# Two layers of attention and experts: blended rows, a third group of expert tiles, respaced preparation, router earlier

## The reference, cut to what matters

```python
# layer 0: causal linear attention (16 heads of 8) and a mixture of 8 experts, 2 of them per token
xn = layernorm(x)
q, k, v = xn @ Wq.T, xn @ Wk.T, xn @ Wv.T           # rope, then elu + 1 on q and k
y_t = (q_t @ sum_{i<=t} k_i v_i^T) / max(q_t . sum_{i<=t} k_i, eps)
p = softmax(xn @ router_w.T); top two, weights normalised
x = x + y @ Wo.T + sum_e w_e * square(relu(xn @ fc_e.T)) @ proj_e.T + shared expert
# layer 1: softmax attention in chunks of 64 with a gate, and a token-shift feed-forward
xn = layernorm(x)
probs = softmax(q k^T / sqrt(8)), reweighed by a gate that is worked out from their sum
x_prev = xn shifted by one token, the first row zero
xr = mu_r * xn + (1 - mu_r) * x_prev
xk = mu_k * xn + (1 - mu_k) * x_prev
out = sigmoid(xr @ W_r.T) * (square(relu(xk @ W_k.T)) @ W_v.T)
x = x + attention + out
```

## Time and profile before

| | |
|---|---|
| median of the three runs | 1634.32 us (1632.23 to 1635.02) |
| the profiled execution's own time | 1633.0 us |
| its span, first to last instruction | 1631.0 us |
| mean granted TensorE clock | 0.972 of full speed |
| busy, share of the span | PE 89%, DVE 73%, ACT 49%, POOL 34% |
| first layer | 0 to about 542 us |
| expert tiles | about 542 to 850 us |
| second layer | about 850 to 1631 us |

### The profile page before, as it was taken

The page is one execution under the profiler, slowest core; times in us unless marked ns, Lnnn a source line. Parts: engine busy times, 40 slices in busy tenths (PEclk is TensorE's granted clock), DMA queues, the critical chain, the costliest instruction groups (busy, mean ns, idle before and its releaser), DMA issues.

```text
span 1631.0 us, 35341 instructions
## 1 busy us (share of the span) xinstructions
PE 1453.1 (89%) x13152; PEld 942.7 (58%) x13152; DVE 1193.0 (73%) x2666; ACT 800.3 (49%) x1505; POOL 548.2 (34%) x967
## 2 busy tenths in 40 slices
PE   3898998998997799997987899999999999999993
PEld 2666766766665699996973444444444444444441
DVE  4788788788787474464665688888888888888741
ACT  2344444444442333343324566666666666666672
POOL 2432332332322011351116043444444534452123
PEclk9999999999998999999997999999999999999996
DMA  4111111111111576776861444343444443432400
GB/s 113 41 41 47 48 41 47 47 41 47 41 34 43 160 218 213 234 227 181 243 155 54 86 97 86 87 89 85 83 105 105 99 96 80 90 83 54 85 8 13
DMA packets 117035, 152.86 MB, mean 94 GB/s; under 512 B 28788, under 2 KB 81652, under 8 KB 112244
## 3 DMA queue, kind: packets, MB, share of 16 engines
q1 hardware_dynamic: 103944, 120.25, 30.0%
q0 software_dynamic: 12928, 30.43, 6.1%
HBM read 109.01 MB, written 41.09 MB: 92 GB/s over the span
## 4 chain that ended last, share of the span: by engine, by line
PE 48%; DVE 26%; DMA 8%; POOL 6%; issue 5%; ACT 4%; SPq 3%; POOLq 0%; DVEq 0%; ACTq 0%
PE bank L1853 8%; PE bank L1844 8%; DVE P L1139 7%; DMA QT<-shift 6%; DVE nmax L1424 6%; PE bank L1721 5%; PE bank L1892 4%; PE bank L1917 4%; PE bank L1678 2%; PE bank L1755 2%; PE bank L1663 2%; PE bank L1966 2%; PE bank L1862 2%; PE bank L1769 2%; ACT QT L777 1%
## 5 line engine op out<-in xcount | busy, mean ns | idle before, releaser
L1424 DVE TENSOR_REDUCE nmax<-bank 128x1 f32<-128x512 f32 (+3 forms) x704 | 429.5, 632 | 116.7 <-PE bank L1892 110.6
L891 ACT ACTIVATE P<-bank 128x512 f32<-128x512 f32 x640 | 368.8, 597 | 284.6 <-PE bank L1917 282.2
L1892 PE MATMUL bank<-KT,QT 76*128 76x512 bf16 (+3 forms) x1024 | 255.6, 306 | 44.8 <-DVE nmax L1424 40.3
L1917 PE MATMUL bank<-QT,KT 78*128 78x512 bf16 (+3 forms) x1024 | 246.9, 304 | 23.9 <-ACT P L891 12.2
L602 POOL DMA_INDIRECT xs_d<-xn,idx x128 | 125.0, 976 | 320.5 <-DVE idx L1119 281.1
L1892 PEld LDWEIGHTS bank<-KT,QT 76*128 76x128 bf16 x1024 | 87.4, 98 | 221.1 <-DVE nmax L1424 134.2
L1721 PE MATMUL bank<-P,V 128*32 128x512 f32 (+3 forms) x2048 | 192.3, 449 | 0.0
L1139 DVE TENSOR_TENSOR P<-bank,early_w 128x512 f32<-128x512 f32 x256 | 158.8, 683 | 44.3 <-PE bank L1678 44.3
L859 ACT ACTIVATE hr<-bank 128x512 f32<-128x512 f32 x144 | 86.0, 597 | 179.4 <-PE bank L1844 179.4
L1394 DVE TENSOR_TENSOR hT<-hr 128x512 f32<-128x512 f32 x144 | 99.1, 692 | 87.0 <-ACT hr L859 84.6
L1917 PEld LDWEIGHTS bank<-QT,KT 78*128 78x128 bf16 x1024 | 98.4, 99 | 99.6 <-ACT P L891 39.2
(11 more groups left out here) (224 smaller groups left out, 2293.2 us busy)
## 6 DMA issues: line engine op xcount, KB each, us to landing
P<-in_fc SPq DMA_DIRECT2D x72, 256.0 KB, 2.7
P<-in_proj SPq DMA_DIRECT2D x72, 256.0 KB, 3.1
QT<-parts_d SPq DMA_DIRECT2D x96, 192.0 KB
parts_d<-parts SPq DMA_DIRECT2D x32, 384.0 KB, 2.7
P<-xs_d SPq DMA_DIRECT2D x72, 128.0 KB, 2.9
ys_d<-P POOLq DMA_DIRECT2D x72, 128.0 KB, 3.3
KT<-parts_d SPq DMA_DIRECT2D x64, 128.0 KB
KT<-parts_d SPq DMA_DIRECT2D x32, 192.0 KB
```

Of the source, the lines that this page charges most:

```text
L891: nc.scalar.activation(P[s % 2][:, u, :], bank[k % 2][:, :], ACT.Exp, scale=float(DH) ** -0.5).then_inc(s_sb, 1)
L1424: nc.vector.tensor_reduce(nmax[:, j, h:h + TWO * nh - 1:TWO], max_bank(n, k)[:, 0:nh * w].rearrange("p (h w) -> p h w", h=nh), AX.X, ALU.m ...
L1892: ins = pe.matmul(max_bank(n, k)[:, i * w:(i + 1) * w], QT[n.p][0:MROWS, h, j * 128:(j + 1) * 128], KT[n.p][0:MROWS, h, 0:w], start=True, ...
L1917: ins = pe.matmul(bank[k % 2][:, c:c + n], KT[b.p][0:SROWS, h, 128 * kb:128 * kb + 128], QT[b.p][0:SROWS, h, 128 * kb:T], start=True, stop ...
```

## The change

Four edits, together in one diff.

1. r and k are worked out from blended rows. ACT scales the rows before by 1 - mu (`scale_before`, units (3, 2) and (3, 4) of the pass before), DVE adds mu times the rows (`blend_rows`, after maxima 38 and 41), and `r_rows` and `k_rows` take one matmul per block, not two. The blends lie in `ee[1]` and `t2[1]`. For FIRST both are made in tiles 56 to 58. `wmix` and its four operations go.
2. Tiles are in three groups: the first 4 of each expert, the next 2, the rest. The six first tiles of an expert hold all rows of the first three batches. POOL gathers the third batch in tiles 52 to 59, DVE combines it in tiles 63 to 66, and the gather after the last tile goes. The plan grows: `planning` has steps 0 to 15, with `rows_ready` at step 14 instead of 11; SP waits for a fourth `plan_ready` at its tile 11.
3. The preparation of FIRST and SECOND in tiles 48 to 58 is respaced: `mid2` and `low2` each one or two tiles later, one part per tile, SECOND's turn, products and splits two to three tiles later.
4. In the first layer `router(b+1)` comes before `y_out(b, 0)` and `states(b+1)`.

```diff
-AHEAD_TILES = 4
+AHEAD_TILES = (0, 4, 6)
-GATHER0, COMBINE0, MAX0 = 33, 41, 57
+GATHER0, COMBINE0, MAX0, GATHER2, COMBINE2 = 33, 41, 57, 52, 63
-        wmix = t2[0][:, :].rearrange("p (k d) -> p k d", k=4)
+        blend = [ee[1], t2[1]]
...
 # SP, tile
-                if k == 2 * TB - 1:
-                    sp.wait_ge(plan_ready, 3)
+                if k in (2 * AHEAD_TILES[1] - 1, 2 * AHEAD_TILES[2] - 1):
+                    sp.wait_ge(plan_ready, 3 if k < 2 * AHEAD_TILES[1] else 4)
-                if k == COMBINE0 + 18:
+                if k == COMBINE0 + 21:
                     store_parts2(SECOND)
...
 # POOL, tile
+                if k == GATHER2:
+                    for p in range(TB):
+                        pool.wait_ge(ys_stored[p], 16 * (E * AHEAD_TILES[2] // TB))
+                if k is not None and GATHER2 <= k < GATHER2 + 2 * J:
+                    gather(FIRST + 2, [k - GATHER2])
-                if k == COMBINE0 + 6:
+                if k == COMBINE0 + 9:
                     ln_root(SECOND)
...
             pool.wait_ge(ey_ps, NTILES)
-            gather(FIRST + 2)
...
 # ACT
+            def scale_before(n, c):
+                if within(n + -1):
+                    act.wait_ge((r_ps, k_ps)[c], n.at(1, -L2))
+                else:
+                    act.wait_ge(setup2, 6)
+                nc.scalar.activation(blend[c][:, :], xnT[n.p][:, 0:T], ACT.Copy, scale=omu[:, c:c + 1]).then_inc(scaled, 1)
...
 # ACT, tile
                 if k == COMBINE0 + 7:
                     hi2(FIRST, 1)
-                    mid2(FIRST, 0)
-                if k == COMBINE0 + 8:
-                    mid2(FIRST, 1)
+                if k in (COMBINE0 + 8, COMBINE0 + 9):
+                    mid2(FIRST, k - COMBINE0 - 8)
+                if k == COMBINE0 + 10:
                     evac_v2(FIRST)
-                if k == COMBINE0 + 12:
-                    hi2(SECOND, 1)
-                    mid2(SECOND, 0)
+                if k in (COMBINE0 + 13, COMBINE0 + 14):
+                    hi2(SECOND, k - COMBINE0 - 13)
+                if k in (COMBINE0 + 15, COMBINE0 + 16):
+                    mid2(SECOND, k - COMBINE0 - 15)
+                if k in (COMBINE0 + 15, COMBINE0 + 16):
+                    scale_before(FIRST, k - COMBINE0 - 15)
...
 # ACT, body2
+                        if at in ((3, 2), (3, 4)) and after:
+                            scale_before(b + 1, u // 2 - 1)
...
 # DVE, planning
                 if k == 0:
                     bounds(1)
-                if k == 1:
-                    inside(1)
-                if k == 2:
-                    row_terms(1)
-                if k == 3:
+                    bounds(2)
+                if k in (1, 5):
+                    inside(1 + k // 5)
+                if k in (2, 6):
+                    row_terms(1 + k // 5)
+                if k in (3, 7):
                     expert_terms()
                     more_tiles(0)
                 if k == 4:
                     more_tiles(1)
-                    other_tiles()
-                if k == 5:
+                    other_tiles(known, ahead)
+                if k == 8:
+                    more_tiles(1)
+                    other_tiles(ahead, NTILES)
+                if k == 9:
                     row_steps()
-                if k in (6, 9):
-                    rows_above(ebase[:, 0, :] if k == 6 else base_b)
-                if k in (7, 10):
-                    rows_moved(step_a if k == 7 else step_b)
-                if k in (8, 11):
-                    rows_summed(k == 11)
+                if k == 10:
+                    rows_above(ebase[:, 0, :])
+                    rows_moved(step_a)
+                if k == 11:
+                    rows_summed(0)
+                    rows_above(base_b)
                 if k == 12:
+                    rows_moved(step_b)
+                    rows_summed(1)
+                if k == 13:
+                    rows_above(base_c)
+                    rows_moved(step_c)
+                if k == 14:
+                    rows_summed(2)
+                if k == 15:
                     second_layer_consts()
...
 # DVE, body of the first layer
+                if not last:
+                    router(b + 1)
                 y_out(b, 0)
                 if not last:
                     states(b + 1)
-                    router(b + 1)
                     router_pick(b + 1)
...
 # DVE
+            def blend_rows(n, c):
+                dve.wait_ge(scaled, n.at(2, c + 1 - 2 * L2))
+                nc.vector.scalar_tensor_tensor(out=blend[c][:, :], in0=xnT[n.p][:, 1:T + 1], scalar=mu[:, c:c + 1], in1=blend[c][:, :],
+                                               op0=ALU.mult, op1=ALU.add).then_inc(blended, 1)
...
 # DVE, tile
-                if k == COMBINE0 + 8:
-                    low2(FIRST, 0)
-                if k == COMBINE0 + 9:
-                    low2(FIRST, 1)
+                if k in (COMBINE0 + 9, COMBINE0 + 10):
+                    low2(FIRST, k - COMBINE0 - 9)
+                if k is not None and COMBINE2 <= k < COMBINE2 + 4:
+                    combine(FIRST + 2, (k - COMBINE2) // 2, range(2 * (k - COMBINE2) % J, 2 * (k - COMBINE2) % J + 2))
-                if k == COMBINE0 + 7:
+                if k == COMBINE0 + 9:
                     ln_moments(SECOND, False)
-                if k == COMBINE0 + 8:
-                    ln(SECOND, False)
-                if k in (COMBINE0 + 12, COMBINE0 + 13):
-                    residue2(SECOND, k - COMBINE0 - 12)
+                if k in (COMBINE0 + 10, COMBINE0 + 11):
+                    ln(SECOND, False, range(2 * (k - COMBINE0 - 10), 2 * (k - COMBINE0 - 9)))
+                if k in (COMBINE0 + 14, COMBINE0 + 15):
+                    residue2(SECOND, k - COMBINE0 - 14)
+                if k in (COMBINE0 + 16, COMBINE0 + 17):
+                    low2(SECOND, k - COMBINE0 - 16)
+                if k in (COMBINE0 + 16, COMBINE0 + 17):
+                    blend_rows(FIRST, k - COMBINE0 - 16)
...
 # DVE, body2
-                    if m in (2, 3, 4, 5) and front:
+                    if m in (2, 3, 4, 5) and front and not b.less(L2 + 1):
+                    if m in (38, 41) and after:
+                        blend_rows(b + 1, (m - 38) // 3)
...
 # PE
-                pe.wait_ge(setup2, 10)
-                pe.matmul(W5[:, :], wmix[:, 3, :], xnT[n.p][:, 1:T + 1], start=True, stop=False)
-                pe.matmul(W5[:, :], wmix[:, 2, :], xnT[n.p][:, 0:T], start=False, stop=True).then_inc(k_ps, 1)
+                pe.wait_ge(blended, n.at(2, 2 - 2 * L2))
+                pe.matmul(W5[:, :], wrkv[:, 1, :], blend[1][:, :], start=True, stop=True).then_inc(k_ps, 1)
...
+                pe.wait_ge(blended, n.at(2, 1 - 2 * L2))
                 for j in range(J):
-                    for shift_ in (1, 0):
-                        ins = pe.matmul(W6[:, j * 128:(j + 1) * 128], xnT[n.p][:, shift_ + j * 128:shift_ + (j + 1) * 128], wmix[:, shift_, :],
-                                        start=(shift_ == 1), stop=(shift_ == 0))
+                    ins = pe.matmul(W6[:, j * 128:(j + 1) * 128], blend[0][:, j * 128:(j + 1) * 128], wrkv[:, 0, :], start=True, stop=True)
...
-                if k == COMBINE0 + 8:
+                if k == COMBINE0 + 9:
                     v_rows(FIRST)
-                if k == COMBINE0 + 10:
+                if k == COMBINE0 + 12:
                     turn_xn(SECOND, False)
-                if k in (COMBINE0 + 11, COMBINE0 + 12):
-                    q_rows(SECOND, k - COMBINE0 - 11)
+                if k in (COMBINE0 + 13, COMBINE0 + 14):
+                    q_rows(SECOND, k - COMBINE0 - 13)
```

73 lines of the change are left out of this document (33 added, 40 removed).

## The result

| | before | after |
|---|---|---|
| median of 4 runs, us | 1634.0 (1632.2 to 1635.0) | 1576.6 (1572.7 to 1578.4) |
| profiled execution, its own time, us | 1633.0 | 1576.8 |
| its span, us | 1631.0 | 1575.1 |
| PE / DVE / ACT busy, us | 1453.1 / 1193.0 / 800.3 | 1423.8 / 1218.9 / 820.9 |

The ratio is 0.9633, 95% interval 0.9604 to 0.9662: 57 us faster. Forecast were 47 us and 1587.1, with a range down to 1572. The measured time lies inside it, on the good side.

What follows compares the result with a forecast made beforehand. PE was taken to bound first layer and plain tiles, with second-layer passes beginning when shift rows land. -16.5 + 13.4 - 10 + 0.5 - 13 - 21.6 = -47.2 from 1634.3 gave 1587.1 us, range 1572 to 1606.

Steps and rivals of the forecast that it cites:

- Router: First layer: filling DVE's 1.20 us of idle time before the states shortens 15 batches by 1.1 us each, -16.5 us.
- Plan in more steps: Expert tiles: the longer plan makes DVE late, stalls PE at tile 15 and slows its start, a loss of 13.4 us.
- (b): SP's tile 15 waits for rows_ready, now step 14; loads queue behind it, so PE stalls 10.6 us before its fc.
- (c): After the stall at tile 15 PE starts slowly at a low clock; 1.6 us added.
- (a): Planning steps 10 to 13 take DVE 2.5 to 2.8 us against 1.9 free; its lateness costs PE 1.2 us.
- Rival A: The stall at tile 15 is small because the loads catch up; 13.4 becomes 3, total 1577 us; chance 0.12.
- Respacing: Tiles 46 to 57: casting a tile behind the residue removes waits of ACT and PE, -10 us, bounds 4 and 13.5.
- Third batch: Second layer's first pass: gathering the third batch early cuts it from 61.9 to 48.1 us; -13 us taken.
- Rival C: Early gather works only partly, tiles 50 to 57 transfer-bound; half of 13 and 10 lost, +11.5, 1599 us; chance 0.18.
- Blended rows: Second layer: PE saves 2.0 us, blends let 0.6 through; 1.4 us in 14 passes plus 2.0 in the last, -21.6.
- Rival B: Second layer: DVE takes back most of the blends' gain, leaving 0.5 us a pass; +12.6, 1600 us; chance 0.18.
- Rival D: Second layer: scales and blends enter each pass in full, saved matmuls were covered; 2.8 x 15 = 42, 1651 us; chance 0.03.

## Why the prediction was right, point by point

**Router: right in mechanism, too small by 10 us.** The step that failed is "15 batches x 1.1". The regular batch gave 1.31, somewhat over the 1.1 read from the 1.20 row. The rest was in the view but not used: I took one batch for all, and five of fifteen were 0.3 to 1.8 us longer, four of them because the clock fell after PE's 1.84 us wait. Undoing this edit alone costs 25.8 us. The upper bound of 27, read as "PE gets all its waiting back", happened to cover it, which was luck: PE's waiting fell by 21.8 us, and most of the rest are the four batches in which the clock no longer falls.

**Plan in more steps: right in (b) and (c), (a) by luck.** (a) The fc of tiles 7, 8, 11 and 12 came 4.40, 3.80, 4.35 and 3.80 us behind the one before, where it had been 4.25, 3.81, 3.73 and 3.73: 0.8 in sum, forecast 1.2. But the cause was another than the forecast's. DVE did fall behind, its copy of tile 13 ends 5.74 us after the fc of tile 14 starts, where it had been 4.13; PE lost nothing by it, tiles 12 to 14 start 3.73 to 3.80 us apart. What PE lost stands at tile 11, behind SP's fourth wait for the plan, to which the forecast had given nothing "beyond the tenths seen there": 0.7 us. (b) Stall before the fc of tile 15, the tile behind SP's long wait: 13.21 - 3.73 = 9.5, forecast 10.6. Rows ready was met within 0.3 us; from there to the last weight issue the queue needed 2.99 us, not the 4.24 of the row before, which is the whole difference. (c) Slow clock behind it: tile 15 took 6.59, so 2.9, forecast 1.6; its window shows 0.57. The row that I had used to size it, eight products after 2.13 us, was too short a reading: the whole tile ran slow. The prediction cites the Trainium skill, page "TensorE: Matmul & The Clock Gate", section "Loop structure matters more than you think", for the rule that matmuls behind a transfer wait run cold. Tile 15 agrees, with a transfer wait of 6.89 us ahead of it. Tile 49, which the prediction gave as its witness, is no case of that rule: PE had waited 2.13 us for ACT there, not for a transfer. Up to the fc of tile 14 the other tiles gave 1.5 back, which makes 11.6. Rival A falls.

**Respacing: right.** 9.0 against 10 in its stretch, and 9.1 when undone on another chip. Behind it, between tile 57 and the second layer, 2.3 us were lost against 0.5 forecast; which edit they belong to is open.

**Third batch: right, size 3.7 short.** First pass 47.2, forecast 48.1, and 63.9 before by these marks, where I had taken 61.9 from others. The landing of the shift rows in it was 7.06 us, not 9.59: the 1.9 us that I added for a slow landing were not owed. Undone: 16.4. Rival C, which halved this and the respacing, falls.

**Blended rows: right for clean passes, 7 us short in the profile.** 1.5 a pass at the full clock against 1.4, so the sum of the steps (2.0 from PE, 0.6 let through) stands; in the last but one, without gathers, it is 2.0, the upper bound, on all four chips. The last batch's products gave 2.1 of 2.0. The sum, -14.3 instead of -21.6, misses by one pass of 53.5 us. What the forecast left out is POOL's root, which now holds DVE in six of the 14 passes. Rival B (0.5 a pass, DVE takes the rest back) is wrong on the first chip. On chips where DVE pauses its size fits roughly (6 to 14 us in 15 passes), but by way of the clock.

**Rival D** would have needed 1.7 us of growth in every pass; one of them grew, the one of 53.5 us.

**Not in the forecast:** 3.6 us between the 16th state sums and the first tile. The run with the router moved back needs 57.1 there where its neighbours need 55.1 to 55.4, so about half of it is the router's.

The errors were of one sign at the first layer, behind it and at the first pass (-9.9, -3.6, -3.7), of the other in the passes (+7.4). The closeness of the total owes something to that.

## What to carry to other kernels

When a wait is set later, list what is queued behind the waiting instruction, and date the last issue it releases: that gave 9.5 us within 1.1 here, and moving the wait behind the loads that did not need it removed it (11 us in its stretch on all three chips tried, and in the total on the two where both kernels ran). Read every repetition of a loop, not one: the odd batches show what a wait costs beyond its own length, when the clock falls behind it. The blends moved work from PE to an engine busy 38 of 46 us; they gave 1.5 to 2.0 us a pass where that engine ran without gaps and 0.4 to 0.9 where it didn't, so compare such an edit on more than one chip. When a pass gets shorter, look at what was ready just in time before, here POOL's root.

The version to keep is the changed kernel with SP's waits at its tiles 32 and 33. It has the lowest ratio of its chip on all three where it ran, 0.9682, 0.9721 and 0.9698; on the first chip it was not run, and its time there, 1576.6 - 11 = 1565, is an estimate from tiles 14 to 16.

## What was not expected of the hardware

**A pause of DVE that comes and goes with the chip.** On the second, third and fourth chip DVE stands 3.6 to 3.7 us in each of 13 batches in a row ahead of the same cut of the attention tiles (line 1154), and 2 to 5 us in every middle pass ahead of a row maximum. In the batches only half of that is the pause: on the first chip DVE stands 1.87 us at the same place in every batch, waiting for PE, so about 1.8 us are new. No rolled loop is at work there: both layers are written out pass by pass, and only tiles 16 to 31 of the expert tiles are rolled. The profile finds no releaser in the program ("remote", "issue"). On the first chip neither kernel shows such a wait without a releaser. Timeline of DVE, then of ACT and PE, in a pass of the run with SP's waits later, second chip:

```profile
1135.65 0.47 DVE L1003 BATCH_NORM_STATS2 stats<-rope 128x6 f32<-128x128 f32 x2
1139.16 0.69 DVE L1458 TENSOR_REDUCE nmax<-bank 128x1 f32<-128x512 f32 x1 [3.03 <-remote]
```

```profile
1140.56 0.60 ACT L897 ACTIVATE P<-bank 128x512 f32<-128x512 f32 x1 [5.75 <-remote]
```

```profile
1139.91 0.34 PE L1928 MATMUL bank<-KT,QT 76*128 76x384 bf16 x1 [2.51 <-DVE nmax L1458]
```

And the windows of that pass, cut where PE resumes and where the clock has recovered:

```profile
1128.78:1139.91 11.13, 8.28 (x72) 4.66 (x68) 6.93 (x19) 3.88 (x7) 7.78 (x9) 1.00 0.71 139
1139.91:1147.92 8.01, 6.83 (x26) 2.63 (x27) 4.74 (x12) 4.16 (x8) 2.24 (x7) 0.59 0.16 37
1147.92:1179.98 32.06, 29.84 (x226) 12.95 (x225) 28.41 (x53) 22.89 (x43) 9.79 (x25) 1.00 0.35 76
```

A pause of 3 us makes a pass 6.4 us longer (51.2 against 44.8). PE's busy time grows from 41.75 to 44.95, because the clock is granted at 0.59 for 8 us after the pause; the other 3.2 are idle. That a wait costs about twice its length was seen after the 1.84 us waits on the first chip too. The change is worth 57 us on the first chip and 38 and 43 on the third and fourth ((1 - 0.9786) x 1761.6 and (1 - 0.9758) x 1762.4). The blends account for some of the difference, with 6 and 14 us in place of about 20; how the rest divides is not shown, since the kernel before has a trace from the first chip alone. What causes the pause was not found, nor whether it goes with the chip or with something else that differed between those executions. The expert tiles hardly know it: 3.73 us a tile and 111.95 for tiles 16 to 45 in all fourteen profiles.
